# Reordering VectorE's seven operations per turn in a software-pipelined graph-attention loop

## The reference: what is computed

```python
k = layer_norm(x_node @ Wk); v = layer_norm(x_node @ Wv); q = layer_norm(x_node @ Wq)
ke = layer_norm(x_edge @ Wke); ve = layer_norm(x_edge @ Wve)
rel_k = layer_norm(concat([ke, k[src]]) @ relk_W + relk_b)
qk = sum(q[dst] * rel_k, -1) / 4
lse = log(segment_sum(exp(qk - m[dst]), dst)) + m            # m: segment maximum
rel_v = layer_norm(concat([ve, v[src]]) @ relv_W + relv_b)
h = (qk - lse[dst]) * rel_v
agg = segment_sum(h, dst)
z = layer_norm(relu(agg @ z_W + z_b))
out = layernorm(x + z)
```

## Time and profile before

| | before |
|---|---|
| device time, median of 3 runs | 3289.94 us (3283.66 to 3290.08) |
| profiled execution, first to last instruction (span) | 3207.3 us |
| TensorE matmul busy | 2937.6 us (92%) |
| TensorE weight load busy | 2485.6 us (77%) |
| VectorE busy | 2978.3 us (93%) |
| ScalarE busy | 2307.1 us (72%) |
| GpSimd busy | 2576.2 us (80%) |
| mean granted TensorE clock | 0.975 |

### The profile page before, as it was taken

How to read it: one execution, slowest core, us unless ns; L and a number is a source line. 1 busy time by engine, 2 the same in 40 slices (tenths; PEclk the granted TensorE clock), 3 DMA queues, 4 the chain that set the end, 5 groups by cost and what they waited for, 6 DMA issues and landing times. The chain is left out here.

```text
span 3207.3 us, 75878 instructions
## 1 busy us (share of the span) xinstructions
PE 2937.6 (92%) x18674; PEld 2485.6 (77%) x18870; DVE 2978.3 (93%) x3387; ACT 2307.1 (72%) x5276; POOL 2576.2 (80%) x2622
## 2 busy tenths in 40 slices
PE   5669999999999999999999999999999999996955
PEld 3358888888888888888888888888888888885633
DVE  7879999999999999999999999999999999996957
ACT  2457777777777777777777777777777777775536
POOL 7768888888888888888888888888888888883773
PEclk9989999999999999999999999999999999999976
DMA  3568887778787778777778777778777777785642
GB/s 86 160 180 237 240 243 240 242 238 243 239 243 239 243 238 243 239 243 240 241 239 244 238 244 238 243 238 244 239 242 240 241 240 241 242 246 176 178 123 76
DMA packets 660921, 715.95 MB, mean 223 GB/s; under 512 B 97993, under 2 KB 554430, under 8 KB 660469
## 3 DMA queue, kind: packets, MB, share of 16 engines
q1 hardware_dynamic: 568201, 499.33, 51.8%
q0 software_dynamic: 84896, 211.42, 21.8%
q10 hardware_dynamic: 7756, 4.43, 0.6%
HBM read 482.62 MB, written 231.46 MB: 223 GB/s over the span
## 5 line engine op out<-in xcount | busy, mean ns | idle before, releaser
L1301 POOL DMA_INDIRECT e_rows<-node_table,e_gcol x1564 | 2093.0, 1338 | 422.2 <-issue 419.9
L1123 PE MATMUL banks<-w_edge,e_eat 128*128 128x240 f32 x6256 | 1435.9, 373 | 57.9 <-DVE e_p L1408 50.6
L1123 PEld LDWEIGHTS banks<-w_edge,e_eat 128*128 128x128 f32 x6256 | 1156.7, 190 | 281.2 <-DVE e_p L1408 207.1
L1116 PE MATMUL banks<-e_h,e_oh 128*128 128x248 f32 x3128 | 805.5, 380 | 9.4 <-ACT e_agg L1200 5.3
L1399 DVE TENSOR_REDUCE e_zs<-e_z 128x96 f32<-128x1440 f32 x391 | 646.1, 1653 | 40.2 <-DVE e_z L1389 7.8
L1209 ACT ACTIVATE e_oht<-banks 128x512 bf16<-128x512 f32 x391 | 233.5, 597 | 476.8 <-remote 240.2
L1116 PEld LDWEIGHTS banks<-e_h,e_oh 128*128 128x128 f32 x3128 | 533.6, 190 | 43.5 <-DVE e_h L1416 6.2
L1200 ACT ACTIVATE e_agg<-banks 128x496 f32<-128x496 f32 x782 | 455.3, 582 | 95.7 <-PE banks L1116 95.7
L1408 DVE TENSOR_TENSOR e_p<-banks,e_yr 128x960 f32<-128x960 f32 x391 | 448.8, 1148 | 3.3 <-PE banks L1123 3.3
L1416 DVE TENSOR_TENSOR e_h<-e_p,e_zw 128x960 f32<-128x960 f32 x391 | 448.9, 1148 | 1.2 <-POOL e_zw L1314 1.2
L1371 DVE TENSOR_TENSOR e_p<-e_p,e_rows 128x960 f32<-128x960 f32 x391 | 449.1, 1149 | 0.0
(11 more groups left out here) (413 smaller groups left out, 2596.6 us busy)
## 6 DMA issues: line engine op xcount, KB each, us to landing
tile_sums<-e_agg SPq DMA_DIRECT2D x391, 496.0 KB
e_q<-q_by_rank SPq DMA_DIRECT2D x1564, 96.0 KB
e_ea<-in_edge_attr SPq DMA_DIRECT2D x390, 256.0 KB
e_rows<-node_table,e_gcol POOLq DMA_INDIRECT x1564
edge_lse<-t_lse_sb SPq DMA_DIRECT2D x14, 448.0 KB, 3.6
edge_qk<-e_qkt SPq DMA_DIRECT2D x130, 48.0 KB
node_table<-n_tb SPq DMA_DIRECT2D x24, 240.0 KB, 2.8
n_x<-in_x SPq DMA_DIRECT2D x24, 128.0 KB, 2.3
```

The source lines that it names most:

```text
L1116: last = nc.tensor.matmul(agg_ps[:, (j % 2) * AW:(j % 2 + 1) * AW], oh[:, x % OR, j, :], hh[:, x % HR, j, :, :].rearrange("p h e -> p (h e ...
L1123: last = nc.tensor.matmul(out_ps[:, j // 2, (j % 2) * 2 * HC:(j % 2 + 1) * 2 * HC], eat[:, x % 4, j * P:(j + 1) * P], t["w_edge"][:, at:at ...
L1301: g.indirect_dma_start(out=rows[:, k, j, :], out_offset=None, in_=table, in_offset=bass.IndirectOffsetOnAxis(ap=gcol[:, kb, at:at + 1].bit ...
```

## The change

VectorE's seven steps in a turn are written in another order. No instruction is added or removed, each keeps its group, its waits and its signals, and the other engines' programs are the same.

```diff
             def body(c, i, loop):
-                x = c - 5
-                if is_group(x, loop):
-                    ...
-                    dve.wait_ge(s_ga[x % RR], 64 * use(x, i, RR))
-                    dve.wait_ge(s_p, n + 1)
-                    v.tensor_tensor(out=p[...], in0=p[...], in1=rows[...], op=ALU.add).then_inc(s_pt, 1)
                 x = c - 9
...
                     v.tensor_tensor(out=hh[:, x % HR, :, :, 2 * C], in0=qk0[:], in1=z[:, x % ZR, :, 2 * H:3 * H, C], op=ALU.add).then_inc(s_qk, 1)
-                x = c - 6
-                ...query product, then_inc(s_pq, 1)
-                x = c - 6
-                ...1440-column sums, then_inc(s_z, 1)
                 x = c - 4
...
                                     op=ALU.mult).then_inc(s_p, 1)
+                x = c - 6
+                if is_group(x, loop):
+                    n, k = UNROLL * i + x, x % PR
+                    dve.wait_ge(s_pt, n + 1)
+                    dve.wait_ge(s_qx, n + 1)
+                    if loop or x >= ZR:
+                        dve.wait_ge(s_z, n - ZR + 1)
+                        dve.wait_ge(s_qk, n - ZR + 1)
+                    v.tensor_tensor(out=z[:, x % ZR, :, 2 * H:3 * H, :], in0=p[:, k, :, :, 0, :],
+                                    in1=qx_ps.rearrange("p (t h d) -> p t h d", t=TILES, d=D), op=ALU.mult).then_inc(s_pq, 1)
+                x = c - 5
+                ...row addition, then_inc(s_pt, 1)
+                x = c - 6
+                if is_group(x, loop):
+                    n = UNROLL * i + x
+                    dve.wait_ge(s_psq, n + 1)
+                    dve.wait_ge(s_pq, n + 1)
+                    ...
+                    v.tensor_reduce(out=zs[:, x % WR, :, :], in_=z[:, x % ZR, :, :, 0:C], axis=AX.X, op=ALU.add).then_inc(s_z, 1)
                 x = c - 9
```

More of the change, by code:

```diff
@@ L1365, in body @@
             def body(c, i, loop):
-                x = c - 5
-                if is_group(x, loop):
-                    n, k = UNROLL * i + x, x % PR
-                    dve.wait_ge(s_ga[x % RR], 64 * use(x, i, RR))
-                    dve.wait_ge(s_p, n + 1)
-                    v.tensor_tensor(out=p[:, k, :, :, :, 0:C].rearrange("p t h k c -> p (t h k) c"), in0=p[:, k, :, :, :, 0:C].rearrange("p t h k c -> p (t h k) c"),
-                                    in1=rows[:, x % RR, :, :].rearrange("p t (h c) -> p (t h) c", c=C), op=ALU.add).then_inc(s_pt, 1)
                 x = c - 9
@@ L1411, in body @@
                                     op=ALU.mult).then_inc(s_p, 1)
+                x = c - 6
[10 more added lines that the diff above has]
+                if is_group(x, loop):
+                    n, k = UNROLL * i + x, x % PR
+                    dve.wait_ge(s_ga[x % RR], 64 * use(x, i, RR))
+                    dve.wait_ge(s_p, n + 1)
+                    v.tensor_tensor(out=p[:, k, :, :, :, 0:C].rearrange("p t h k c -> p (t h k) c"), in0=p[:, k, :, :, :, 0:C].rearrange("p t h k c -> p (t h k) c"),
+                                    in1=rows[:, x % RR, :, :].rearrange("p t (h c) -> p (t h) c", c=C), op=ALU.add).then_inc(s_pt, 1)
+                x = c - 6
+                if is_group(x, loop):
+                    n = UNROLL * i + x
+                    dve.wait_ge(s_psq, n + 1)
+                    dve.wait_ge(s_pq, n + 1)
+                    if loop or x >= WR:
+                        dve.wait_ge(s_zl, n - WR + 1)
+                        dve.wait_ge(s_qk0, n - WR + 1)
+                    v.tensor_reduce(out=zs[:, x % WR, :, :], in_=z[:, x % ZR, :, :, 0:C], axis=AX.X, op=ALU.add).then_inc(s_z, 1)
                 x = c - 9
```

## The result

| | before | changed |
|---|---|---|
| median | 3286.91 us (3283.66 to 3290.08, 4 runs) | 3474.52 us (3457.43 to 3485.20, 4 runs) |
| ratio | | 1.0551, 95% interval 1.0522 to 1.058 |
| span of the profiled execution | 3207.3 us | 3455.6 us |
| setup: start to first score addition | 236.8 us | 285.5 us |
| steady turn of VectorE | 6.95 us | 7.40 us |

The changed kernel is 5.5% slower; 3156 us were forecast. Executions of one kernel come in two kinds here, over the whole program and for many runs on end: before takes 3208 us in the one and 3283 in the other, and the profile of before in this table is of the first kind, all else in it of the second.

What follows compares the result with a forecast made beforehand. VectorE's full 6.95 us turn was taken as the bound. Pitches of 6.57 (VectorE) and 6.56 (TensorE) plus 0.03 gave 6.60; 384 turns save 134 us: 3207.3 - 134 = 3073, plus 82.6, 3156 us; range 3120 to 3235.

Steps and rivals of the forecast that it cites:

- What bounds the kernel: Edge loop: VectorE runs seven back-to-back instructions, 6.95 us a turn, 384 turns, 83% of the span; TensorE is next bound.
- the self-waits: VectorE waits on its preceding instruction after score addition and product; removing these saves 0.21 + 0.17 = 0.38 us a turn.
- The 0.03 allowance: Added to the 6.57 us pitch because two engines so close at times wait for each other: 6.60.
- Second projection: On TensorE, its wait for VectorE's scaling goes, saving 0.42 us; TensorE's own pitch becomes 6.52, on average 6.56.
- GpSimd: Its gathers are stretched by VectorE operations; unheld its turn is 5.70 us, room 0.87 at 6.57, so nothing is added.
- The half of the rule of the Trainium skill: A running GpSimd gather would block VectorE's weighted values; as a rival, turn 7.30, +134 us, 3424 us, 4%.
- The base of the sum: Predicted span 3073 us plus the 82.6 us around it, between traced span and median 3289.9, gives 3156 us.
- I cost both at nothing: Scaling's later input from TensorE and ScalarE's later work after the row addition were taken to fit, adding no time.
- The room of 0.42 us: TensorE's turn may start between 0.22 and 0.64 us ahead of VectorE's; 0.18 with the 1.14.
- The rivals: Alternatives to the forecast: half the gain 18%, no change 6%, GpSimd as the bound 9%, VectorE held by a gather 4%.
- Half the gain: Short score addition followed no faster than 0.34, or TensorE waits for ScalarE's later copies: saving 65, 3225 us, 18%.
- The pause of 0.42: TensorE's hold ahead of the second projection, waiting for the scaling; its removal was counted as 0.42 us saved a turn.

Runs made afterwards that it cites:

- c3_after: The changed kernel run again, no further edit, with signals on time: 3049.95 us, ratio 0.951 to the kernel before at 3208.07 us.
- e0_before: The kernel before, unedited, run again with its own profile where signals are late: 3283.49 us beside before at 3281.99 us.
- c0_before: The kernel before, unedited, run again with its own profile, signals on time: 3208.00 us, ratio 1.0001.
- after: Profile of the changed kernel from the first result, signals late: span 3455.6 us, median of the runs 3474.52 us against 3286.91 before.
- f3_row_first: Against before, VectorE order row addition, score addition, scaling, query product, sums of squares, 1440-column sums, weighted values; signals on time: 3182.56 us, ratio 0.992.

## Why the prediction was wrong, by its steps

- *What bounds the kernel, and the self-waits:* right. Where signals are on time, 0.12 (forecast 0.13) and 0.59 (0.61) stand in place of 0.34 and 0.78, the turn is 6.54 (6.57, then 6.60 with the allowance), and 3208 became 3050: 158 saved for 134. The 0.03 allowance was not needed; between 600 and 2400 us of `c3_after` no wait of VectorE is listed.
- *Second projection, GpSimd:* right there. The wait of the earlier trace rows is gone, one gather a turn is stretched, none holds VectorE. The half of the rule of the Trainium skill ("SBUF — State Buffer", section "Who interferes with whom") that spoke against the change did not show in `c3_after` either: its weighted values start at 1503.24, at the usual pitch, under a gather that runs from 1502.95 to 1503.96. The prediction also put the rule too strongly: the page states the block for a whole instruction of VectorE's two-port modes, and of two inputs in SBUF it says that they contend with GpSimd's reads.
- *The base of the sum:* wrong. The 82.6 us between span and median were taken for launch and end. They are 2; the rest, some 80 us, was a sign that the timed executions were not like the traced one. Without it the same sum gives 3073 + 2 = 3075 us for the kind of the trace, where 3050 was measured.
- *"I cost both at nothing":* the step that failed. The room of 0.42 us between TensorE and VectorE was measured against a signal time of 0.04, read from the one trace. In the executions that were timed, TensorE's signals come 0.8 to 3.2 us late in the loop, and what is over the room stands in every turn, as that step itself says: first sums 0.87 later than in `c3_after` (1.62 after TensorE's turn start for 0.75), and 6.54 + 0.87 = 7.41, with 7.40 measured. Its sign of being wrong, VectorE waiting at the scaling for the second projection, is what the profile shows.
- *The rivals:* none had this. "Half the gain" names the place, TensorE waiting for ScalarE's later copies, but prices it as gain lost and not as a slower turn, since all rivals went by instruction durations. The pause of 0.42 that the change removes was booked as pure gain. (A slip without effect: a pitch of 6.52 gives 3125 us, not 3127.)
- Open: what holds the signals back. Fewer TensorE instructions and fewer DMAs both lessen it; neither a pause nor a rate of instructions explains it. The traces of late executions also hold fewer than half of the semaphore updates (41259 in `e0_before`, 83135 in `c0_before`), so the recording itself may have a part; no run was without it.

## What to carry to other kernels

Subtract span from time before using either: if what is left differs from the few us of other runs, the trace is not of the execution that is timed. A schedule whose two fullest engines wait for each other within 0.4 us lives on signal latency; before taking the slack between them away, ask what happens if the signals of one come 2 us late. Moving only the scaling gave 2.9% with signals on time and 1.7% with them late; it is the only order here that beats before in both.

## What the hardware showed unexpectedly

- Finished signals of TensorE can come 0.8 to 3.2 us after its matmuls end, three within 0.15 us (`after`), and in the setup up to 14.9 us after, while TensorE is idle (`e0_before`). In a late execution before's setup takes 281 us for 234 with the same code.
- 16 TensorE instructions fewer per turn (91 to 75), at the same number of columns, won 270 us or more in a late execution (3157.70 against 3427.36) and 1 us with signals on time.
- Two neighbouring VectorE operations with both inputs in SBUF can hold one gather for 3.11 us instead of 1.01 (`f3_row_first`).
